# Graph network layer: the second layer of the node update computed with its SiLU rows as the stationary operand

## The reference, cut to what matters

```python
h   = maximum(layernorm(x), 0)
e   = silu(concat(h[row], h[col], dist) @ eW1 + eb1)      # one row of 128 for each edge
e   = silu(e @ eW2 + eb2)
agg = segment_sum(e, row)                                 # 12500 x 128
out = silu(concat(h, agg) @ nW1 + nb1) @ nW2 + nb2        # nW2: 128 x 64, nb2: 64
return x + out
```

## Time and profile before

| | |
|---|---|
| three runs | 3041.51, 3042.06, 3044.26; median 3042.06 |
| profiled execution, first to last instruction | 3042.3 |
| granted PE clock, mean over the span | 0.986 |
| busy, share of the span | PE 87%, PEld 68%, DVE 70%, POOL 66%, ACT 53% |
| chain that ended last | PE 81%, issue 11%, ACT 4%, DVE 3%, DMA 1% |
| first `outer` of the tail starts | 2907.2 |
| last DVE instruction (`finish(24)`) starts | 3037.40 |

### The profile page before, as it was taken

One profiled execution on the slowest core, in us unless ns is written; L12 is line 12 of the kernel. 1 busy time (PEld: TensorE's weight loads), 2 busy tenths in 40 slices (PEclk: granted clock), 3 DMA queues, 4 the chain that ended last, 5 costly groups with the idle time before them and its releaser, 6 DMA issues.

```text
span 3042.3 us, 77490 instructions
## 1 busy us (share of the span) xinstructions
PE 2652.8 (87%) x21703; PEld 2068.1 (68%) x21704; DVE 2125.5 (70%) x7337; ACT 1601.7 (53%) x3366; POOL 2012.3 (66%) x2075
## 2 busy tenths in 40 slices
PE   7899999999688888888888888888888888888899
PEld 4555555555477777777777777777777777777776
DVE  8999999997566666666666666666666666666665
ACT  3677777777344444444444444444444444444455
POOL 1254444445677777777777777777777777777772
PEclk7999999999799999999999999999999999999999
DMA  3011111111222222222222222222222222222343
GB/s 94 20 40 27 39 28 39 34 34 30 48 59 59 60 57 59 59 60 59 58 59 59 60 60 58 58 60 59 59 59 59 59 59 58 58 59 55 77 120 103
DMA packets 366054, 171.78 MB, mean 56 GB/s; under 512 B 289494, under 2 KB 330126, under 8 KB 365934
## 3 DMA queue, kind: packets, MB, share of 16 engines
q0 software_dynamic: 69600, 123.49, 15.4%
q1 hardware_dynamic: 274142, 36.29, 7.8%
q10 hardware_dynamic: 22192, 10.53, 1.2%
HBM read 139.11 MB, written 31.04 MB: 56 GB/s over the span
## 4 chain that ended last, share of the span: by engine, by line
PE 81%; issue 11%; ACT 4%; DVE 3%; DMA 1%; POOL 0%; ACTq 0%; SPq 0%; DVEq 0%; POOLq 0%
PE bk L1208 16%; PE bk L1228 15%; PE bk L1219 13%; PE bk L1206 9%; PE bk L1196 5%; PE bk L1071 4%; PE bk L1217 3%; PE bk L1105 3%; PE bk L1137 2%; PE bk L1059 2%; PE bk L1060 2%; PE bk L1239 1%; ACT BIG L1354 1%; PE bk L1099 1%; PE bk L1274 1%
## 5 line engine op out<-in xcount | busy, mean ns | idle before, releaser
L554 POOL DMA_INDIRECT GA<-q_d,IX x1758 | 1671.5, 951 | 545.4 <-issue 533.3
L920 DVE SCALAR_TENSOR_TENSOR GA<-c_bc,EW,GA 128x128 f32<-128x128 f32 x1758 | 558.5, 349 | 432.7 <-DMA GA<-q_d,IX 429.2
L929 DVE TENSOR_TENSOR BIG<-bk,BIG 128x128 f32 x1758 | 511.4, 291 | 345.1 <-issue 156.4
L1206 PE MATMUL bk<-identf,GA 128*128 128x128 f32 x1758 | 501.2, 285 | 253.8 <-issue 240.3
L1208 PE MATMUL bk<-OHS,P 128*128 128x128 bf16 x5274 | 695.8, 225 | 0.1
L1443 ACT ACTIVATE ED<-bk,eb1c 128x512 f32<-128x512 f32 x440 | 302.1, 687 | 703.0 <-PE bk L1208 698.7
L1208 PEld LDWEIGHTS bk<-OHS,P 128*128 x5274 | 501.3, 96 | 111.3 <-issue 0.2
L1228 PE MATMUL bk<-ED 128*128 128x128 f32 x3516 | 504.7, 287 | 0.0
L519 POOL DMA_INDIRECT rec_d<-BIG,GA x208 | 246.8, 1187 | 376.9 <-issue 285.6
L1219 PEld LDWEIGHTS bk<-W,ED 128*128 128x128 f32 x3516 | 464.8, 193 | 24.3 <-issue 7.6
L1206 PEld LDWEIGHTS bk<-identf,GA 128*128 128x128 f32 x1758 | 247.5, 141 | 321.7 <-issue 297.2
(11 more groups left out here) (247 smaller groups left out, 2761.9 us busy)
## 6 DMA issues: line engine op xcount, KB each, us to landing
GA<-q_d,IX POOLq DMA_INDIRECT x1758, 2.5
q_d<-QS SPq DMA_DIRECT2D x14, 448.0 KB, 3.1
u_d<-QS ACTq DMA_DIRECT2D x98, 64.0 KB
OHS<-u_d SPq DMA_DIRECT2D x18, 256.0 KB, 3.1
rec_d<-ED SPq DMA_DIRECT2D x16, 220.0 KB, 9.6
RW<-rec_d SPq DMA_DIRECT2D x110, 32.0 KB
rec_d<-BIG,GA POOLq DMA_INDIRECT x208, 2.4
HT<-hT_d ACTq DMA_DIRECT2D x99, 32.0 KB
```

The costliest lines, as they stand in the source:

```text
L554: e.indirect_dma_start(G[k % 4 * U + u], None, q_d, bass.IndirectOffsetOnAxis(ap=IX[g // BG % 2][:, k * U + u:k * U + u + 1], axis=0))\
L920: ins = e.scalar_tensor_tensor(out=G[k % 4 * U + u], in0=c_bc[:, :], scalar=ew[:, w:w + 1], in1=G[k % 4 * U + u], op0=ALU.mult, op1=ALU.add)
L929: e.tensor_tensor(AGG[:, ds(v, P)], banks[6 + k % 2][:, u * P:(u + 1) * P], AGG[:, ds(v, P)], ALU.add).then_inc(s["ad"], 1)
L1206: e.matmul(z, G[k * U + u], identf[:, :], is_transpose=True, start=True, stop=False)
```

## The change

```diff
-        nb2c = sb("nb2c", [NF, 1], fp32)
+        nb2r = sb("nb2r", [P, 4 * NF], fp32)
-        OT = [sb(f"OT{k}", [NF, 512], fp32) for k in range(2)]
@@ sync: loads of the weights
-                         (nb2c[:, :], nb2.rearrange("(n a) -> n a", a=1))):
+                         *((nb2r[:, j * NF:(j + 1) * NF], nb2.rearrange("(a n) -> a n", a=1).broadcast_to([P, NF]))
+                           for j in range(4))):
@@ vector, tensor, scalar: the waits for the weights
-            e.wait_ge(s["w"], 16 * 11)
+            e.wait_ge(s["w"], 16 * 14)
@@ vector
+            def biased(c):
+                w, rows = size(c)
+                t = XR[c % 6][0:rows, :]
+                e.wait_ge(s_fy[c % 6], 16 * (c // 6 + 1))
+                e.tensor_tensor(t, t, nb2r[0:rows, :], ALU.add).then_inc(s["fb"], 1)
             def finish(c):
-                e.wait_ge(s_fy[c % 6], 16 * (c // 6 + 1))
+                e.wait_ge(s["fb"], c + 1)
                 e.wait_ge(s["ft"], c + 1)
...
                     weigh(g // 8, g % 8)
+                if 0 <= c - 6 < NF2:
+                    finish(c - 6)
                 if g - 2 < NG:
                     add(g - 2, (g - 2) % 4)
                 if g % BG == BG - 1 and g // BG + 2 < NG // BG:
                     decode(g // BG + 2, g // BG % 2, g // (2 * BG) + 1, g + 1)
-                if 0 <= c - 6 < NF2:
-                    finish(c - 6)
+                if 0 <= c - 4 < NF2:
+                    biased(c - 4)
@@ tensor
             def outer(c):
                 e.wait_ge(s["fd"], c + 1)
-                ge(e, s["fc"], c)
-                e.matmul(banks[3][0:NF, 0:w], nW2s[:, :], F1[c % 3][:, 0:w], start=True, stop=True).then_inc(s["fu"], 1)
-            def turned(c):
-                e.wait_ge(s["fc"], c + 1)
                 ge(e, s["fo"], c)
-                cols = OT[c % 2][:, 0:w].rearrange("p (n j) -> p j n", j=4)
+                cols = F1[c % 3][:, 0:w].rearrange("p (n j) -> p j n", j=4)
                 for j in range(4):
-                    last = e.matmul(banks[5][0:rows, j * NF:(j + 1) * NF], cols[:, j, :], identf[0:NF, 0:NF],
-                                    is_transpose=True, start=True, stop=True)
+                    last = e.matmul(banks[5][0:rows, j * NF:(j + 1) * NF], cols[:, j, :], nW2s[:, :], start=True, stop=True)
                 last.then_inc(s["ft"], 1)
-                if 0 <= c - 6 < NF2:
-                    turned(c - 6)
                 if 0 <= c - 5 < NF2:
                     outer(c - 5)
@@ scalar
-                ge(e, s["fu"], c - 2)
+                ge(e, s["ft"], c - 2)
                 e.activation(F1[c % 3][:, 0:w], UR[c % 4][:, 0:w], ACT.Silu, bias=nb1c[:, :]).then_inc(s["fd"], 1)
-            def columns(c):
-                e.wait_ge(s["fu"], c + 1)
-                ge(e, s["ft"], c - 1)
-                e.activation(OT[c % 2][:, 0:w], banks[3][0:NF, 0:w], ACT.Identity, bias=nb2c[:, :]).then_inc(s["fc"], 1)
-                if 0 <= c - 5 < NF2:
-                    columns(c - 5)
```

More of the change, by code:

```diff
@@ L271, in gnn @@
                  "xm sq h t1 ht pq p1 r1 r2 p2c p3 rcp ep dk qc fin htd qd ini scat0 scat1 scat2 scat3 "
-                 "oh st ad tp z1 z2 ap oT of e1 e2 zero var rt hd fz fu ft fc fo fd outs one").split()
+                 "oh st ad tp z1 z2 ap oT of e1 e2 zero var rt hd fz fb ft fo fd outs one").split()
         s = {n: sem("s_" + n) for n in names}
@@ L1272, in outer @@
                 e.wait_ge(s["fd"], c + 1)
-                ge(e, s["fc"], c)
-                e.matmul(banks[3][0:NF, 0:w], nW2s[:, :], F1[c % 3][:, 0:w], start=True, stop=True).then_inc(s["fu"], 1)
-            def turned(c):
-                w, rows = size(c)
-                e.wait_ge(s["fc"], c + 1)
                 ge(e, s["fo"], c)
-                cols = OT[c % 2][:, 0:w].rearrange("p (n j) -> p j n", j=4)
+                cols = F1[c % 3][:, 0:w].rearrange("p (n j) -> p j n", j=4)
                 for j in range(4):
-                    last = e.matmul(banks[5][0:rows, j * NF:(j + 1) * NF], cols[:, j, :], identf[0:NF, 0:NF],
-                                    is_transpose=True, start=True, stop=True)
+                    last = e.matmul(banks[5][0:rows, j * NF:(j + 1) * NF], cols[:, j, :], nW2s[:, :], start=True, stop=True)
                 last.then_inc(s["ft"], 1)
             e.wait_ge(s["uc"], NB)
-            for g in range(TAIL, FINAL + NF2 + 6):
+            for g in range(TAIL, FINAL + NF2 + 5):
                 c = g - FINAL
@@ L1488, in silu3 @@
                 e.wait_ge(s["fa"], c + 1)
-                ge(e, s["fu"], c - 2)
+                ge(e, s["ft"], c - 2)
                 e.activation(F1[c % 3][:, 0:w], UR[c % 4][:, 0:w], ACT.Silu, bias=nb1c[:, :]).then_inc(s["fd"], 1)
-            def columns(c):
-                w, rows = size(c)
-                e.wait_ge(s["fu"], c + 1)
-                ge(e, s["ft"], c - 1)
-                e.activation(OT[c % 2][:, 0:w], banks[3][0:NF, 0:w], ACT.Identity, bias=nb2c[:, :]).then_inc(s["fc"], 1)
-            for g in range(TAIL, FINAL + NF2 + 5):
+            for g in range(TAIL, FINAL + NF2 + 4):
                 c = g - FINAL
```

## The result

The changed kernel takes 3046.04 (median of 20 runs, 3042.16 to 3049.27), the kernel before 3041.14 in the same sessions (20 runs). The ratio is 1.0015, 95% interval 1.0009 to 1.0021: slower, by 2.7 to 6.4, where 18.6 faster was forecast. Two executions of later sessions were slow ones (3178.46 of the kernel before, 4579.41 of the changed kernel); medians and ratios here are of the fast ones alone.

What follows compares the result with a forecast made beforehand. PE was taken to set the tail's pace; 13.8 from its rounds plus 4.8 after mB(439) made 18.6, off the span 3042.3 giving 3023.7, the median 3023.5. Range 3019.5 to 3029.5, forecast's chance 0.80.

Steps and rivals of the forecast that it cites:

- What bounds the kernel: PE carries 81% of the chain and alone sets the tail's pace until mB(439), POOL's floor of 5.07 a round close.
- The removed 1.72, gap of 0.09 included: Tail round of 6.00: the stretch from mB's end to the next mA goes, with the gap from changing array shape.
- I take 0.120, the nearest row: 8 x 0.120 = 0.96: Outer's eight load-and-stream pairs in a tail round, priced from turned's strided pairs; round 5.24, gain 13.8 over 19 rounds.
- bound of 0.268: Upper limit for one pair of outer: the load laid bare, 0.213 as recorded, plus its stream of 0.055.
- rival (b): Outer's strided load laid bare, 0.268 a pair: round 6.42, time 3053.0; decides from 0.214 a pair; chance 0.02.
- The other engines cost 0: Tail rounds: ACT loses columns, DVE gains biased (0.43) but stays under 5.24, POOL doesn't bind; all cost 0.
- Rival (c): Each biased holds POOL's gathers up 0.43, a group takes 5.50: 10.6 gained in place of 13.8, time 3026.7; chance 0.06.
- The way out, 4.8 gained: From the end of mB(439) to the end of finish(24): 13.2 in place of 18.04, steps of 1.8.
- Rival (e), the clock: Late drain at half clock: pairs bound by 64 columns, 0.110, below 0.120; costs under 1, in the range; no separate chance.
- Start-up, 0: Four broadcast loads delay the first load of x by up to 4.7, covered since rows are read at 78.2: cost 0.
- Sum: Whole kernel: 13.8 + 4.8 = 18.6 off the profiled span 3042.3 gives 3023.7; median 0.2 below, 3023.5.
- the prediction's own slope: How the gain follows outer's pair price: 1.5 either way for each 0.01 of a pair.

Runs made afterwards that it cites:

- sorted kernel: Changed kernel with ACT's SiLU writing F1 sorted, so outer's stationary operand is contiguous: 3022.59 against 3040.17 for the kernel before, ratio 0.9944; again 3021.33, ratio 0.9944.
- loads alone: Kernel before with only the four broadcast loads of the bias added, result unused: 3558.36 against 3554.37 on a slower chip, ratio 1.0009 (1.0000 to 1.0018).

## Why the prediction was wrong

- **What bounds the kernel**: right for the tail. From the changed to the sorted kernel, with nothing of PE's but the loads of `outer` altered, the stretch from `mB(420)` to `mB(439)` fell from 116.35 to 98.95. Nearly all of that is PE's own work; the 1.0 above 19 x 5.16 - 0.11 = 97.9 comes with seven waits of `weigh` for a gather, so POOL's floor had come close. The reading of 81% as PE's hold on the whole span was not sound: in the long loop of the kernel before, POOL starts a gather every 1.25 and waits for no one (its 80 waits above are the 0.3 between two gathers), `weigh` waits for the gathers, and PE has waits. It did no harm, as the change lies in the tail.
- **The removed 1.72, gap of 0.09 included**: right. 6.00 - 1.72 + 1.87 = 6.15; 6.13 was measured.
- **"I take 0.120, the nearest row: 8 x 0.120 = 0.96"**: this is the step that failed, the price of a pair of `outer`. It measured 8 x 0.233 = 1.87. The row was a transpose, and the runs show that a transpose at that step pays half of what a plain fp32 load pays (0.120 against 0.233, on 64 rows as on 128). I had matched step, columns and stream, and let the mode pass as if it were no difference. The same text held the rule that spoke against it, the 16-byte line, and booked the 0.120 as its whole price. The contiguous pair of `mC` (0.111) would have been right for a contiguous operand, and is what the sorted kernel has (0.112).
- **The bound of 0.268 and rival (b)**: the mechanism of (b) is the one that came, its price was too high. (b) was to decide from 1.72 / 8 = 0.215 a pair (the text has 0.214), and 0.233 lies just beyond. But the load isn't laid bare: with 128 columns streamed the pair is still 0.233. It hides the stream beneath itself. The recorded 0.213 wasn't its duration either; the plain load is recorded at 0.327. I gave (b) 0.02, against the one rule at hand that spoke for it.
- **The other engines cost 0**: right in the tail. `biased` is 0.415 (0.43 forecast), and PE waits for neither `weigh` nor POOL there. Rival (c), POOL held up by `biased` for its 0.43 each time, doesn't show: gathers stay at 0.944 at the median between 2905 and 2980. A few of them are longer than before, 1.37 at most against 1.11, most of these with no `biased` beside them.
- **The way out, 4.8 gained**: sized with the same wrong pair, 1.1 came. With pairs of 0.112 it is 13.2 and 13.7 from `mB(439)`, where 13.2 from its end, 13.8 from its start, was forecast; steps of 1.75 against 1.8, but for one of 1.98.
- **Rival (e), the clock**: it fell as (e) had it, and cost next to nothing. The window from 3036 to 3037 of the changed kernel (granted clock third from last):

```profile
...
3036.00:3037.00 1.00, 1.00 (x6) 1.00 (x5) 0.00 (x0) 0.00 (x0) 0.00 (x0) 0.50 0.31 102
...
```

At this lower level (1.2 GHz) the strided pairs still stood 0.233 apart, and those of the last chunk, 53 columns, (1.08 - 0.311) / 7 = 0.110, as (e) had worked out for the stream.

- **Start-up, 0**: open, see the loads alone.
- **Sum**: I set the median 0.2 below the profiled span. The later executions take 1.8 more than their spans (3045.74 against 3043.9), so the profiled one before will have been about 3 above its median. It changes no sign.

The forecast of 18.6 for pairs of 0.120 is borne out by the kernel that has them near that: sorted gained 17.6 and 18.9 by the medians, 17.0 by the ratio. Its pairs of 0.112 would by the prediction's own slope be worth 19.8; that 1.0 is part of the difference.

## What to carry to other kernels

Which operand is stationary decides whose layout the weight load reads. In a plain fp32 matmul a load at a step of four elements costs twice its contiguous price, so sort the operand when it is written, where an idle engine can do it for nothing. When a price is taken from a nearest row, the mode of the instruction counts as much as its shape; a row that differs in mode gives a bound, not a value. A gain on one engine counts only where that engine sets the pace: shorter rounds of PE were worth 14 in the tail on the fast chips, and little on the chip where `mB`'s result reached ACT late. A chain's shares don't tell which engine that is, when the same kernel gives PE 79% in one execution and POOL 52% in another; who waits for whom does.

## What the runs showed of the hardware

- A plain fp32 weight load costs about 1.8 ns for each 16-byte piece touched in a row, with a floor of 0.11 for 128 columns, whatever the rows (64 or 128) and the stream (64 or 128 columns).
- The strided load costs 0.233 at a granted clock of 1.00 and of 0.50 alike.
- At a step of 16 bytes a transpose's load costs 0.120 and a bf16 load about 0.06, against 0.233.
- ACT's SiLU over 128 x 512 fp32, read at a step of four elements from SBUF, takes 1.23 in place of 0.71.
- The same kernel before ran at 3040 on two chips of this kind, at 3509 and at 3554 on two others. On the 3509 one ACT starts 1.66 after the recorded end of `mB` where it is 0.04 on a fast one, and POOL's added wait is for that same `mB`.
